# A graph-layer kernel on one core: all eight batches written out, in place of a loop of two turns in the middle

## The reference

```python
x: [8, 1024, 128] float32; adj: [8, 1024, 1024] int32
mask = adj != 0
idx  = the first 25 neighbours of each node (lowest column numbers)
agg  = max over those neighbours of x[neighbour], feature by feature
agg  = where(degree <= 25, maximum(agg, 0), agg)
h    = concatenate([x, agg], axis=-1)
y    = x + relu(h @ W + b)
out  = layernorm(y, axis=-1)
```

## Time and profile before

| | us |
|---|---|
| median of 3 runs | 598.47 (597.78 to 600.49) |
| the profiled execution | 601.36 |
| its span, first to last instruction | 599.6 |
| mean granted TensorE clock | 0.972 |
| DVE busy | 532.0 (89%) |
| PE busy | 497.7 (83%) |
| ACT busy | 396.1 (66%) |
| POOL busy | 289.9 (48%) |

### The profile page before, as it was taken

The page is one execution under the profiler, slowest core; times in us unless marked ns, Lnnn a source line. Parts: engine busy times, 40 slices in busy tenths (PEclk is TensorE's granted clock), DMA queues, the critical chain, the costliest instruction groups (busy, mean ns, idle before and its releaser), DMA issues.

```text
span 599.6 us, 14483 instructions
## 1 busy us (share of the span) xinstructions
PE 497.7 (83%) x4480; PEld 340.1 (57%) x4544; DVE 532.0 (89%) x973; ACT 396.1 (66%) x751; POOL 289.9 (48%) x462
## 2 busy tenths in 40 slices
PE   1357998989987998879976899789987999889982
PEld 0125576566664576556753567555764667556762
DVE  5647999999999999999996899999999999998884
ACT  3362577548974788747975479757887579546654
POOL 2643365157533675147633366335751576336710
PEclk9998999899999999999997899999999999889996
DMA  8983245464535755455537456355444553021102
GB/s 254 223 226 87 78 134 126 101 149 120 134 91 146 143 141 127 125 119 159 131 96 151 103 112 134 98 146 138 140 129 118 140 148 69 2 60 33 52 10 72
DMA packets 91817, 71.40 MB, mean 119 GB/s; under 512 B 63651, under 2 KB 80294, under 8 KB 91686
## 3 DMA queue, kind: packets, MB, share of 16 engines
q1 hardware_dynamic: 85286, 56.77, 38.7%
q0 software_dynamic: 6400, 13.12, 8.0%
HBM read 50.99 MB, written 4.19 MB: 92 GB/s over the span
## 4 chain that ended last, share of the span: by engine, by line
PE 39%; DVE 31%; issue 13%; DVEq 9%; DMA 4%; ACT 2%; SPq 1%; POOL 0%; POOLq 0%
PE pair L1043 33%; DVE part L786 13%; DVE hot L781 4%; DMA adj_sb<-in_adj 4%; DVEq L856 3%; DVE g_feat L859 3%; DVE g_val L827 2%; PE misc L1088 2%; DVE agg_t L886 2%; DVEq L925 2%; PE misc L1089 1%; DVEq L993 1%; DVEq L902 1%; DVE hot_high L781 1%; PE p_V L1083 1%
## 5 line engine op out<-in xcount | busy, mean ns | idle before, releaser
L1043 PE MATMUL pair<-hot,x_part 128*128 128x128 bf16 (+3 forms) x3120 | 411.3, 280 | 47.4 <-DVE part L786 27.9
L1043 PEld LDWEIGHTS pair<-hot,x_part 128*128 128x128 bf16 x3120 | 237.6, 99 | 152.8 <-issue 41.0
L786 DVE TENSOR_REDUCE part<-pair 128x128 f32<-128x1024 f32 (+1 forms) x256 | 279.6, 1099 | 36.1 <-PE pair L1043 28.6
L484 POOL DMA_INDIRECT g_feat<-in_x,g_idx x200 | 194.5, 972 | 132.2 <-issue 84.5
L531 POOL TENSOR_TENSOR y_sb<-relu_sb,x_sb 128x128 f32<-128x128 f32 x64 | 29.9, 468 | 152.7 <-ACT relu_sb L657 152.2
L603 ACT ACTIVATE V<-p_V 128x512 bf16<-128x512 f32 x98 | 57.7, 589 | 69.7 <-remote 60.7
L781 DVE TENSOR_SCALAR hot<-V 128x1024 bf16<-128x1024 bf16 x224 | 81.1, 383 | 0.0
L631 ACT ACTIVATE hot<-V,first_bias 128x1024 bf16<-128x1024 bf16 x56 | 63.9, 1142 | 24.8 <-PE pair L1043 24.8
L596 ACT ACTIVATE mask<-adj_sb 128x1024 bf16<-128x1024 uint32 x56 | 58.7, 1048 | 20.7 <-DMA adj_sb<-in_adj 20.7
L646 ACT ACTIVATE hot<-distance,one 128x1024 bf16<-128x1024 bf16 x56 | 63.9, 1140 | 0.2
L639 ACT ACTIVATE distance<-V,second_bias 128x1024 bf16<-128x1024 bf16 x56 | 63.6, 1135 | 0.0
(11 more groups left out here) (88 smaller groups left out, 396.0 us busy)
## 6 DMA issues: line engine op xcount, KB each, us to landing
adj_sb<-in_adj SPq DMA_DIRECT2D x56, 512.0 KB
g_adj<-in_adj SPq DMA_DIRECT2D x8, 512.0 KB
x_sb<-in_x SPq DMA_DIRECT2D x8, 512.0 KB, 3.8
out<-y_sb SPq DMA_DIRECT2D x7, 512.0 KB, 5.0
g_feat<-in_x,g_idx POOLq DMA_INDIRECT x200
maskT<-mask SPq DMA_TRANSPOSE x56
out<-y_sb SPq DMA_DIRECT2D x1, 448.0 KB, 3.0
w_sb<-in_W SPq DMA_DIRECT2D x1, 128.0 KB, 7.2
```

The lines of the kernel that those rows point to most:

```text
L484: pool.indirect_dma_start(out=g_feat[w][:, k, :], out_offset=None, in_=x_rows, in_offset=bass.IndirectOffsetOnAxis(ap=g_idx[w][:, k:k + 1] ...
L786: dve.tensor_reduce(part[:, par(q, s), :, p], slots_of(q, s, p).rearrange("f k i -> f i k"), AX.X, ALU.max).then_inc(s_used, 1)
L1043: last = pe.matmul(dst, x_part[:, q, part_no, kb], one_hot, start=(first and part_no == 0), stop=(final and part_no == PARTS - 1))
```

## The change

`run` no longer takes the engine and no longer opens a loop. It calls `step` eight times with Python numbers, the last time with `last` set. All five engines get it. Nothing inside `step` is edited.

```diff
@@ -330,16 +330,11 @@
         SEQUENCE = [*range(1, MT), 0, MT]
         ORDER = {t: SEQUENCE.index(t) for t in range(NT)}
 
-        def run(eng, step):
-
-
-            step(0, 0, False)
-            step(0, 1, False)
-            with eng.Fori(1, B // 2 - 1) as i:
-                step(i, 0, False)
-                step(i, 1, False)
-            step(B // 2 - 1, 0, False)
-            step(B // 2 - 1, 1, True)
+        def run(step):
+
+
+            for batch in range(B):
...
@@ -1181,7 +1176,7 @@
                 count(0, 0, s)
             pe.wait_ge(s_const, 16)
             pe.wait_ge(s_bstep, 9)
-            run(pe, step)
+            run(step)
             linear_main(B // 2 - 1, 1, MT)
```

More of the change, by code:

```diff
@@ L331, in build @@
         ORDER = {t: SEQUENCE.index(t) for t in range(NT)}
-        def run(eng, step):
-            step(0, 0, False)
-            step(0, 1, False)
-            with eng.Fori(1, B // 2 - 1) as i:
-                step(i, 0, False)
-                step(i, 1, False)
-            step(B // 2 - 1, 0, False)
-            step(B // 2 - 1, 1, True)
+        def run(step):
+            for batch in range(B):
+                step(batch // 2, batch % 2, batch == B - 1)
         def following(i, q):
@@ L419, in _ @@
                     transpose_mask(*ahead(0, 0, 1, n - 1))
-            run(sp, step)
+            run(step)
             store(B // 2 - 1, 0)
@@ L581, in _ @@
             split_bias()
-            run(pool, step)
+            run(step)
             residual(B // 2 - 1, 1, 0)
@@ L754, in _ @@
                     split_mid(0, 0)
-            run(act, step)
+            run(step)
             relu(B // 2 - 1, 1, 0)
@@ L1008, in _ @@
             first_V(MT)
-            run(dve, step)
+            run(step)
             merge(B // 2 - 1, 1, MT)
```

## The result

The written-out kernel takes 593.56 us (592.16 to 593.94, 4 runs) beside 599.48 us for the kernel before (597.78 to 602.07, 4 runs): a ratio of 0.9893, interval 0.9851 to 0.9936. It was measured a second time later, on six runs of 591.06 to 594.49 us with median 593.01, beside 17 runs of the kernel before with median 602.58 (598.60 to 604.32): 0.9856, interval 0.9823 to 0.9889. The kernel before varies more from run to run than the other does. The gain is about 6 to 9.5 us, and both intervals hold the values from 6.7 to 8.9 us.

The account below looks back on a forecast made before the run. VectorE and TensorE, both near full and handing buffers to each other, were taken as the bound. Gains of 4.4 + 3.8 + 1.1 = 9.3 us off the median 598.47 gave 589.2 us, range 585.5 to 594.5.

Parts of the forecast that it names:

- The bound and the cuts: VectorE and TensorE, both near full, bound the kernel; VectorE's level writes, once a batch, cut the span into batch stretches.
- The turn of the loop: Between batches 3 and 4, VectorE's idle time at the jump back falls from 5.06 to 0.65 us: 4.4 us gained.
- The clock behind the turn: After TensorE's pause at the jump back its matmuls run near half clock; removing this gains 3.8 us, lower end 0.
- yardstick: The 67.2 us stretch, the only one of written-out code alone besides the first, taken as the length without a loop.
- Entry, exit and registers: Entering and leaving the loop, its register operations and separate waits in batches 2 to 5: 1.1 us gained, bounds 0 to 2.3.
- The queues and the text: Loads, transposes and stores on SP, gathers on POOL, and eight written batches instead of six: 0 us.
- Only the pause goes: Rival: the clock falls at batch ends anyway and register work was hidden; gain 4.4 us, time 594.1 us, chance 0.24.
- The pause comes back as a wait for transfers: Rival: behind the former jump back an engine waits for transfers instead; gain about 2 us, time 596.5 us, chance 0.09.
- Slower through forward jumps: Rival: jumps over unused redo code land on unloaded code, 6.3 us each; two landings give 601.8 us, chance 0.05.

Follow-up runs that it names:

- the short loops: Written-out kernel plus, on every engine, a loop of two turns around one do-nothing instruction between batches 3 and 4: 593.35 us, ratio 0.9892 to the kernel before.
- the jumps over 400 and 600: Written-out kernel with VectorE jumping forward over never-executed instructions ahead of batches 2 and 4: 60 and 600 in one kernel, 601.39 us; 200 and 400 in another, 598.85 us.

## Why the prediction was right, and where it wasn't

**The bound and the cuts** held. DVE and PE share the bound, and the pause of either at the turn moves the end: the stretch grows by 4.7 and 4.8 us when each has it alone.

**The turn of the loop, 4.4 us.** Confirmed, from both sides. DVE's idle time at that place fell by 4.8, from 5.06 to 0.26 us, and putting back DVE's loop alone makes the stretch 4.7 us longer. What I didn't see is that PE's loop alone costs as much. I had called DVE's the pause that sets the end. It does when both are there, but PE's stands ready right behind it, and taking away only one of the two would have gained about 0.5 us in that stretch (72.6 less 72.0 or 72.1). In the whole time, by the ratios, it would have been 0.3 to 0.4%, 1.6 to 2.3 us, with intervals that overlap. The overlap of the two pauses, put at little more than 1 us, is about 1.5 (320.3 to 321.75).

**The clock behind the turn, 3.8 us.** In the two stretches where I looked for it the gain came: 8.9 us measured for 4.4 + 3.8 = 8.2 expected. But the term counted the falls of the clock that the turn had caused, and not those that come anyway. The mean granted clock from 100 to 540 us, first before and then after, is the same:

```profile
100.00:540.00 440.00, 387.17 (x3521) 265.32 (x3575) 412.11 (x765) 309.86 (x590) 221.84 (x310) 0.98 0.49 120
```

```profile
100.00:540.00 440.00, 399.07 (x3633) 271.03 (x3632) 417.84 (x778) 315.40 (x604) 224.62 (x315) 0.98 0.50 120
```

The falls moved. In the first profile after the change two of them stand behind the shared buffer's waits at 183 and 453 us, and the stretch around the second grew from 67.1 to 68.9. In the second profile of the same kernel that stretch is 67.7, so the size of this is chance in part. That is the step of the prediction that was mis-sized: the two stretches gained 8.9, of which 4.8 are the pause, and with 1.8 given back the clock was worth about 2.3 us, within the 0 to 3.8 that the text bounded it by. My yardstick of 67.2 us was right for the ends of batches 0, 2, 4 and 6 only. Batches 1, 3 and 5 end with the shared buffer.

**Entry, exit and registers, 1.1 us.** Measured 0.5 us (68.1 + 68.6 less 68.4 + 67.8). The 68.1 that I laid in part on entering the loop is 68.4 and 68.3 in two profiles with no loop there, 67.2 with the short loops, and 67.2 once the buffers rotate. So nothing points at the loop, though what made it 68.1 at a granted clock of 1.00 isn't shown. The lower bound, 0, was the better value: with DVE's loop in place the three stretches without the turn are 0.9 us shorter in sum than written out, and with PE's only those named above are longer.

**The queues and the text, 0 us.** Confirmed by the kernel in which SP, POOL and ACT keep their loops, 594.87 us and a stretch of 67.3.

**The rivals.** Only the pause goes: 594.1 us was its time, and the first comparison's 593.56 is nearer to it than to the forecast's 589.2. Both of its premises came out: the clock falls at other places anyway, and the register work was hidden. Its sign did not: the two stretches became 67.3 and 66.4, not 68.4 and 69.8. More than the pause is gone in the place itself, and something was given back elsewhere. The pause comes back as a wait for transfers: no such wait is there; what came back was a wait for a buffer, out of sight before. The sign that I gave for this rival, PE waiting for DVE 3 us longer at the end of batch 3, was a poor one: PE does wait 2.83 us there, and the stretch is 67.3 us all the same. Slower through forward jumps: it did not happen in this text, where DVE shows no unexplained idle time above 0.46 us between 100 and 540 us. The mechanism is real, though. Two jumps put in by hand cost all of the gain. The rule of the Trainium skill, "Runtime: NRT & Kernel Launch", section Instruction fetch mechanics, that a taken jump whose target isn't held stalls the engine, agrees with the turn's 5.06 us and the packets of code inside the pauses, with the near loop, and with the jumps over 400 and 600. The 3.05 us of the jump over 200 neither supports nor contradicts it, as long as it isn't known where the code lies. The branch times of the Trainium skill, "Advanced Engine Details and Errata", section Control Flow Timing, of about 51 and 108 ns, are near what the short jumps took here, 0.2 us from a branch to the next instruction, and not what the far ones took.

**The size.** 589.2 us was forecast against a median of 598.47 for before, and 593.56 was measured. Part of the gap lies in the median of before, which was 599.48 and 602.58 in the comparisons. As a gain, 9.3 us were forecast, and 5.9, 7.6 and 9.6 were found by the first medians, the two spans and the second medians. The second agreement with 9.3 is luck in part: the spans show the pause as forecast (4.8), and about 2.3 us of the clock's 3.8 and 0.5 of the entry's 1.1.

## What to carry to other kernels

A loop on the engines' registers costs its turns: where all engines are near full, ask of each turn how much code it jumps back over on each engine and which engine is on the path, and write the turns out if there are few. The registers and the waits against them cost nothing that showed here, and the turns of ScalarE and SyncE, with short bodies, took 0.3 us. When a stall is removed, look at what it covered: here a buffer rotation that restarted every second batch only because the loop's code needed it, and once the text was written out, an edit of a few lines made it continuous and gave another 2.3 and 3.4 us in two comparisons.

## What the runs showed of the hardware that I had not expected

In the stretch with the turn, PE's and DVE's pauses cost nearly the same whether one or both are there (4.8, 4.7 and 5.2 us); the whole time, 8.1 us longer with both and 4.4 and 3.4 with one, doesn't bear that out. One and the same turn took 0.3 us on SP and ACT, 2.5 on POOL, 4.7 on DVE and 5.0 on PE, and each loop kept on PE or DVE brought 3 more packets of code. A conditional jump forward took DVE 0.21 us over 60 instructions, 3.05 over 200, 4.42 over 400 and 4.05 + 1.88 over 600. And TensorE's granted clock fell to about half for some 4 us behind waits of 2 to 3 us in some places of some kernels and not in others: the same wait of 2.8 us was followed by 0.62 and 0.57 at two places of one profile and by 1.00 at a third, and by 1.00 at both places in the kernel before.
